# Cross-attention kernel: one exponential a chunk on the scalar engine, the rounded copy of the weights cast by the vector engine one step later

## What is computed

```
h = layer_norm(x)
qh, kh, vh = h @ wq + bq, ctx @ wk + bk, ctx @ wv + bv    # 16 heads of 128
kh, vh = concat(kh, bias_k), concat(vh, bias_v)           # 1501 keys
weights = softmax(qh . kh / sqrt(128))
x = x + (weights . vh) @ wo + bo                          # twice
x = x + gelu(layer_norm(x) @ w_fc1 + b_fc1) @ w_fc2 + b_fc2
```

## Time and profile before

| | |
|---|---|
| median of 3 runs | 1341.99 us (1341.84 to 1342.36) |
| the profiled execution's own time | 1341.05 us |
| its span | 1339.2 us |
| busy share of the span: PE, POOL, ACT, DVE | 94%, 67%, 61%, 57% |
| granted PE clock, mean | 0.983 of full speed |
| chain that ended last: PE, POOL, issue, DVE, ACT | 72%, 8%, 7%, 7%, 4% |

### The profile page before, as it was taken

One profiled execution on the slowest core, in us unless ns is written; L12 is line 12 of the kernel. 1 busy time (PEld: TensorE's weight loads), 2 busy tenths in 40 slices (PEclk: granted clock), 3 DMA queues, 4 the chain that ended last, 5 costly groups with the idle time before them and its releaser, 6 DMA issues.

```text
span 1339.2 us, 27136 instructions
## 1 busy us (share of the span) xinstructions
PE 1257.2 (94%) x8016; PEld 1146.7 (86%) x8016; DVE 769.1 (57%) x1368; ACT 811.8 (61%) x1572; POOL 896.1 (67%) x750
## 2 busy tenths in 40 slices
PE   6999999999999999989799999999999999999897
PEld 5778989898989898978686889898989888889786
DVE  6855556565656565537684555555555555555554
ACT  4655666665656565666383656665666666667554
POOL 4646767676767676668572667676767676766772
PEclk9999999999999999999898999999999999999898
DMA  5401111111111110112250111111111111101131
GB/s 175 129 13 38 56 46 46 46 46 46 46 46 47 45 49 31 34 49 70 83 164 26 36 38 56 41 53 43 58 35 57 34 57 34 57 23 44 49 94 30
DMA packets 30426, 72.69 MB, mean 54 GB/s; under 512 B 3072, under 2 KB 4144, under 8 KB 30368
## 3 DMA queue, kind: packets, MB, share of 16 engines
q1 hardware_dynamic: 30368, 72.01, 17.1%
HBM read 71.52 MB, written 0.48 MB: 54 GB/s over the span
## 4 chain that ended last, share of the span: by engine, by line
PE 72%; POOL 8%; issue 7%; DVE 7%; ACT 4%; DMA 1%; DVEq 1%; POOLq 0%; ACTq 0%; SPq 0%
PE psum L621 30%; PE psum L642 10%; PE psum L644 9%; PE psum L643 9%; PE psum L591 4%; PE psum L675 4%; POOL pt L486 3%; PE psum L653 2%; POOL ctx L436 2%; DVE g_prod L1091 1%; POOL qs L451 1%; DMA w_raw<-weights 1%; PE psum L635 1%; ACT slots L894 1%; PE psum L628 1%
## 5 line engine op out<-in xcount | busy, mean ns | idle before, releaser
L486 POOL TENSOR_TENSOR pt<-slots,pt 125x512 fp32r<-125x512 f32 (+1 forms) x384 | 444.0, 1162 | 243.4 <-ACT slots L894 241.4
L621 PE MATMUL psum<-qs,ctx 128*125 128x384 f32 (+1 forms) x2304 | 542.1, 372 | 18.7 <-POOL qs L451 14.5
L621 PEld LDWEIGHTS psum<-qs,ctx 128*125 128x125 f32 x2304 | 396.0, 187 | 68.2 <-issue 20.8
L642 PE MATMUL psum<-ctx,pt 125*128 125x258 f32 x1344 | 388.1, 289 | 8.7 <-ACT on L900 7.8
L1154 DVE TENSOR_TENSOR t_max<-psum,t_max 125x512 f32<-125x512 f32 (+1 forms) x320 | 199.3, 623 | 322.9 <-PE psum L621 322.8
L643 PE MATMUL psum<-ctx,pt 125*128 125x256 f32 x1344 | 379.6, 282 | 0.0
L644 PE MATMUL psum<-ctx,pt 125*128 125x258 f32 x1344 | 379.3, 282 | 0.0
L925 ACT ACTIVATE slots<-psum 125x512 f32<-125x512 f32 (+1 forms) x384 | 207.8, 542 | 215.6 <-DVE t_max L1154 184.1
L893 ACT ACTIVATE pt<-slots 125x512 fp32r<-125x512 f32 (+1 forms) x384 | 221.4, 577 | 148.9 <-DVE slots L1142 116.3
L642 PEld LDWEIGHTS psum<-ctx,pt 125*128 125x128 f32 x1344 | 253.5, 189 | 25.5 <-ACT on L900 18.1
L643 PEld LDWEIGHTS psum<-ctx,pt 125*128 125x128 f32 x1344 | 254.1, 189 | 5.5
(11 more groups left out here) (84 smaller groups left out, 1037.1 us busy)
## 6 DMA issues: line engine op xcount, KB each, us to landing
nat_stage<-ctx_nat SPq DMA_DIRECT2D x64, 375.0 KB
tr_stage<-ctx_tr SPq DMA_DIRECT2D x64, 375.0 KB, 3.0
w_raw<-weights SPq DMA_DIRECT2D x72, 256.0 KB, 2.7
dk_all<-dk_rows SPq DMA_DIRECT2D x2, 768.0 KB, 6.3
dk_all<-dk_rows SPq DMA_DIRECT2D x2, 256.0 KB, 4.2
xres<-x_rows SPq DMA_DIRECT2D x4, 112.0 KB, 2.3
out_rows<-xres SPq DMA_DIRECT2D x4, 112.0 KB, 1.9
bo<-out_bias SPq DMA_DIRECT2D x1, 336.0 KB, 3.5
```

Of the source, the lines that this page charges most:

```text
L486: nc.gpsimd.tensor_tensor(split_weights(h, LO, c), slot(h, c), as_f32(split_weights(h, HI, c)), ALU.subtract).then_inc(pt_lo, 1)
L621: last = mm(scores(h, k), ctx_tr_chunk(half, a, c), qs[h][:, m, half, 0:R], start=(half, a, m) == terms[0], stop=(half, a, m) == terms[-1])
L642: mm(O_BANK[j][:, 0:D + 2], hi, ctx_nat_hi(c), start=(c == 0), stop=False, skip_group_check=True)
```

## The change

ACT's exponential into `pt` (L893) and its wait on `pv_mm` are taken out. A new DVE function `rounded` casts the exponential from `slots` into the HI part of `pt`, `ROUND_LAG` = 15 steps after the scores. In every step it stands behind `normalized` and ahead of `shifted`. It waits for `exp_done` and `pv_mm` and signals the new semaphore `pt_hi`. POOL's `weights_lo` waits for `pt_hi` instead of `exp_done` and moves from lag 14 to lag 15, in the steps and in the tail.

The parts of the diff below are, in order, the constants, POOL's three, ACT's one and DVE's two.

```diff
-    SUB_LAG, PV_LAG = 14, 17
+    SUB_LAG, ROUND_LAG, PV_LAG = 14, 15, 17
...
                 def weights_lo(b, i, h, c):
-                    pool.wait_ge(exp_done, INIT + l * LAYER_STEPS + b * STEPS + (i + 1))
+                    pool.wait_ge(pt_hi, INIT + l * LAYER_STEPS + b * STEPS + (i + 1))
...
                 def batch_steps(b, first, last):
-                        i, h, c = lagging(k, SUB_LAG)
+                        i, h, c = lagging(k, ROUND_LAG)
...
                 batch_steps(B - 1, False, True)
-                for k in range(SUB_LAG):
-                    i, h, c = lagging(k, SUB_LAG)
+                for k in range(ROUND_LAG):
+                    i, h, c = lagging(k, ROUND_LAG)
...
                 def weights_hi(b, i, h, c):
                     act.wait_ge(sub_done, INIT + l * LAYER_STEPS + b * STEPS + (i + 1))
-                    act.wait_ge(pv_mm, INIT + l * LAYER_STEPS + b * STEPS + (i + 1 - RING))
-                    go(split_weights(h, HI, c), slot(h, c), ACT.Exp)
                     go(slot(h, c), slot(h, c), ACT.Exp).then_inc(exp_done, 1)
...
+                def rounded(b, i, h, c):
+                    dve.wait_ge(exp_done, INIT + l * LAYER_STEPS + b * STEPS + (i + 1))
+                    dve.wait_ge(pv_mm, INIT + l * LAYER_STEPS + b * STEPS + (i + 1 - RING))
+                    V.tensor_copy(split_weights(h, HI, c), slot(h, c)).then_inc(pt_hi, 1)
...
                         if c == 5 and not first:
                             normalized(b - 1, h)
+                        i, ph, pc = lagging(k, ROUND_LAG)
+                        if (i >= 0 or not first) and not (tail and i >= 0):
+                            rounded(b, i, ph, pc)
                         i, ph, pc = lagging(k, SUB_LAG)
                         if (i >= 0 or not first) and not (tail and i >= 0):
                             shifted(b, i, ph, pc)
```

More of the change, by code:

```diff
@@ L227, in build @@
         px_ready, pe_done = sem("px_ready"), sem("pe_done")
-        sub_done, exp_done, pt_lo, pv_mm = sem("sub_done"), sem("exp_done"), sem("pt_lo"), sem("pv_mm")
+        sub_done, exp_done, pt_hi, pt_lo, pv_mm = (
+            sem("sub_done"), sem("exp_done"), sem("pt_hi"), sem("pt_lo"), sem("pv_mm"))
         den_ready, rden_ready, pn_ready = sem("den_ready"), sem("rden_ready"), sem("pn_ready")
@@ L252, in build @@
                     dv_ready, gp_ready, gp_used, q_lo, first_qs_lo, lb_rows_ready, nat_hi, tr_hi, lb_ready, max_done,
-                    mt_reduced, max_ready, px_ready, sub_done, den_ready, rden_ready, pn_ready, on_dve, p80_lo,
+                    mt_reduced, max_ready, px_ready, sub_done, pt_hi, den_ready, rden_ready, pn_ready, on_dve, p80_lo,
                     oth_lo, c_lo, xb_ready],
```

## The result

| | before | after |
|---|---|---|
| median of the runs, us | 1342.03 (4 runs, 1341.84 to 1342.36) | 1356.96 (4 runs, 1356.93 to 1359.97) |
| ratio, 95% interval | | 1.0125 [1.0112, 1.0137] |
| span of the profiled execution, us | 1339.2 | 1355.1 |
| one batch of the loop, us | 65.93 | 66.69 |
| last scores to last product of a layer, us | 26.50 and 26.50 | 29.94 and 29.97 |

The page of the changed kernel answers to the earlier trace rows; its second line is the chain that ended last, by engine.

A forecast was written before the change was run, and what follows sets the result against it. PE, busy 94% of the span, was taken as the bound, waiting late in a batch for POOL's queue. Terms of 5.6, 7.7, 22.4 and 9.2 us, together 44.9 on 1341.05, gave 1386 us; range 1344 to 1408.

The forecast's parts named there:

- Item 3: Start of the next batch: casts and signal waits make POOL's query split later, 1.6 us in 14 places, 22.4 us.
- the queue of POOL had slack that I took for none: Stated sign of being wrong: casts run at the double rate and collide, yet the batch is still 66 us.
- Item 2: Steps 14 to 17: casts meeting POOL's pieces delay step 16's maximum; PE's wait grows 0.55 us in 14 batches, 7.7 us.
- Item 1: Step 13: the new cast stands before the DVE subtraction PE waits for, +0.35 us in 16 batches, 5.6 us.
- Item 4: Tail: a chunk takes 1.45 us as POOL and cast exclude each other; 4.6 us, twice, 9.2 us.
- I count no gain for them by themselves: ACT's 384 removed exponentials, 221.4 us busy, were counted as worth nothing, since ACT has idle time around them.
- The rate and the lock: DVE's cast runs at the double rate, 0.42 or 0.36 us; it and a POOL piece exclude each other for their whole length.
- Rival B: Cast at the single rate, locking nothing: 8.8 us at step 13, -8.4 at the split, 7 a layer in tail; 1355 us, chance 0.12.
- Rival A: POOL reaches each query split 1.3 us sooner, so PE's 14.5 us of waits there vanish: 1333 us, chance 0.13.
- rival C: Waits add up: late maxima hold PE 0.3 us in half of twelve steps a batch, 25 us more: 1411 us, chance 0.10.
- D: Nothing comes of it: POOL's gain at the split and the tail's cost cancel, 1342 us, chance 0.05.

The follow-up runs named there:

- lag15_only: The kernel before with only POOL's weights_lo subtraction moved from lag 14 to lag 15, no cast added: 1339.66 us, ratio 0.9999.
- half_narrow: half_cast with the ring pt at 512 columns instead of 520: 1346.30 us, ratio 1.0054.
- single_rate: The changed kernel with its cast in three parts at the single rate, a gap column between them, ring pt of 520 columns: 1353.99 us, ratio 1.0089.
- half_cast: The changed kernel casting only 3 x 86 or 3 x 64 elements, at the single rate, ring pt of 520 columns: 1344.76 us, ratio 1.0033.
- cast_behind: The changed kernel with DVE's rounded moved behind shifted in each step of the loop: 1398.60 us, ratio 1.0436.
- pool_free: The changed kernel with POOL waiting for the exponential instead of the cast and taking unrounded weights twice, PE waiting for both signals: 1352.41 us, ratio 1.0097.

## Why the prediction was wrong in size

The parts of the sum, each with what it measured:

| item | predicted, us | measured, us |
|---|---|---|
| 1. step 13 | 5.6 | 2.7 (13.15 - 9.75, less 0.7 in the tails) |
| 2. steps 14 to 17 | 7.7 | 1.4 (9.2 - 7.8) |
| 3. start of the next batch | 22.4 | 4.7 (19.2 - 14.5) |
| 4. tail | 9.2 | 6.9 (3.44 + 3.47) |
| sum | 44.9 | 15.7 (span: 15.9) |

**Item 3 failed, and with it most of the 30 us.** Its step was "from 944.19 on POOL has its next piece ready almost without a gap", and a walk that let each collision from there on push the split. The trace had a second release that came at the same time: POOL's context piece at 951.19 starts 0.17 us after DVE's context cast (950.07 + 0.95) and just as its own piece before it ends. `lag15_only` shows that the cast is what holds. So POOL has 1.77 us of slack up to step 20, as soon as one chunk moves behind the split, and only casts that delay DVE's own maximum, or that collide in the pieces behind it, reach PE. That came to 0.5 us a batch where the walk had 1.6, and at the start of two batches it was a gain. The condition that the text itself gave for being wrong, "then the queue of POOL had slack that I took for none", is the case.

**Item 2**: the collisions came as told (casts of 0.71, 0.97 and 1.13 us in steps 14 to 16), but the maximum of step 16 was late by 0.3 us and not by 1.4 (946.99 against 938.85, each from its batch's start). DVE had 1.14 us of idle time left at step 14, and at step 16 the 0.99 us of the earlier trace rows, and both went to the casts. **Item 1** took the cast's duration (0.35); from its start to the start of the subtraction it holds DVE for 0.26 us (938.75 to 939.01). **Item 4** told 4.6 us a layer; the last half took 3.1 us more and the spread ahead of it 0.35. Its chunk came out right (1.45 us told, 1.42 measured) partly by luck, since the reason was another: ACT and DVE in turn, with the lock only 0.4 of the 3.1 us, and 1.0 from POOL's later step.

**"I count no gain for them by themselves"** was false, and its error did not show in the sum, because the walk took the cast's early start for granted: with the exponential left in (`act_twice`) the change costs 4.0%. That it did not show was luck.

**The rate and the lock** were right: minimum 0.35 us, waits up to 1.51 us, and 9.5 us of the result by `half_narrow`. Rival B gave 1355 us and so the nearest time, by a mechanism that the cast's minimum refutes. `single_rate`, which casts as B describes, takes the same time only because the longer cast costs about what the lock does; and the 8.4 us that B wins at the split did not come (14.6 us of waits against 14.5). Rival A failed on POOL's gap, rival C on the absorbed delays, D on the interval. As for the Trainium skill, page "SBUF — State Buffer", section "SBUF: two separate sides": the rule that the loser fully blocks fits the collisions shown here (casts of up to 1.51 us, ending after POOL's piece). The page gives the lock, on DVE's side, to operations in a two-port mode or with two inputs in SBUF; `half_cast`, which is neither, fits with casts of 339 to 424 ns beside the same POOL pieces. The Trainium skill's page "Perfetto Trace Analysis", section "Optimizing Scalar/DVE Operations", says that such an operation is faster on DVE if a faster mode is available. That holds here for the one instruction (a cast of 0.41 us without waits against an exponential of 0.63) and not for the kernel: ACT had the time free, and the move cost 1.25%.

## What to carry to other kernels

Before walking collisions forward through an engine's queue, look for the last point at which that queue waits for another engine, also where the two releases fall together: what is lost ahead of it costs nothing. Of a cast that DVE takes over, ask what it waits for and which signal it stands in front of; with ACT's other exponential left in, the cast cost 37 us more here, the lock cost 9.5 us, and casts longer by 0.2 us 7.5 us. Where PE's clock is lower after a wait, count that too: it was 16 us of `act_twice`'s price. And where PE waits for a short piece at the end of a queue, move that piece first: the split three steps sooner won 1.2%, more than any version of the change.

## What the runs showed of the hardware

- After an idle time of 3.40 us PE's granted clock fell to 0.50, its lower level (1.2 GHz), and the six matmuls behind it took 2.92 us instead of 1.65. In the batch loop the 12 waits of 1.5 us in the change did not do that; of the 14 waits of 2.0 to 2.4 us in `act_twice` eight did. Timeline and windows of `cast_behind`:

```profile
530.75 2.92 PE L622 MATMUL psum<-qs,ctx 128*125 128x512 f32 x6 [3.40 <-POOL qs L452]
```

```profile
530.75:533.70 2.95, 2.95 (x8) 2.25 (x9) 0.14 (x1) 0.00 (x0) 2.51 (x2) 0.50 0.00 0
533.70:538.00 4.30, 4.30 (x32) 4.03 (x31) 2.70 (x7) 1.40 (x3) 1.29 (x1) 0.98 0.00 0
```

- A ring 8 columns wider shortened PE's own instructions from 63.75 to 63.55 us a batch and the kernel by 2.8 us (the change), 2.8 (`half_cast`) and 4.4 (the kernel before with the split at 19). No run tells which tensor's place, `pt`'s own rows or the one behind them, does it.
- POOL's subtraction of 512 columns takes 1148 ns on the mean with the same input twice (`pool_free`), against 1307 in the kernel before with two inputs; the shortest with 384 columns took 821 and 992 ns.
